# Decoder kernel: exponentials three steps ahead in the scan layer, and the last expert layer's first two experts split by ScalarE and VectorE

## The chip, the core and the metric

The kernel is one program on one core of a Trainium2 chip. The core has five engines with a queue of instructions each: TensorE (PE) for matrix products and transposes, VectorE (DVE), ScalarE (ACT), GpSimd (POOL), and SyncE (SP), which here only starts transfers. They wait for each other through semaphores. The metric is the device time of one execution in microseconds (us), the median of some runs.

## The reference

Two sequences of 1024 tokens, 256 channels wide, go through six layers, each behind a layer norm and added to its input. The change touches the first and the last:

```python
# x: (2, 1024, 256)
x = x + L0_attn(layernorm(x))    # a selective state-space scan ("Mamba"), inner width 512, 16 states
x = x + L0_xattn(layernorm(x))   # attention to a context of 77 rows
x = x + L0_ffn(layernorm(x))     # top-1 mixture of 8 experts
x = x + L1_attn(layernorm(x))    # a mixer of several parts
x = x + L1_xattn(layernorm(x))   # attention with sparsemax
x = x + L1_ffn(layernorm(x))     # top-2 mixture of 8 experts

# L0_attn, the scan over time t, for each of 512 channels d and 16 states n:
dA = exp(dt_t * A)
h  = dA * h + dt_t * B_t * x_t
y  = einsum('bdn,bn->bd', h, C_t)

# L1_ffn:
m, sel = top_k(logits, 2)        # masks and two softmaxes give two weights for each token
for e in range(8):
    h = silu(x @ w1[e].T) * (x @ w3[e].T)
    out = out + wte[:, e:e+1] * (h @ w2[e].T)
```

## The kernel before, in words

**The scan layer** (`mamba`, from L226). The 2048 tokens are worked in NK = 4 chunks of 512, and each chunk in NU = 64 steps: 16 states n by CI = 4 groups c of 128 channels. One step is one tile of 128 channels x 512 tokens, and step G of the whole layer passes through four engines:

- ScalarE makes the exponential dA[G] (`decay`, L582), into one of AR = 6 buffers. For that it waits until the scan of step G - 6 has read its buffer. It also makes the B product UT, tokens on the partitions and all 512 channels in a row, in four slices of 128 tokens for a state (`times_b`, L572). The slices for the group of four steps N are made during the four steps of group N - 1; the first of them waits until TensorE has taken the slices of group N - 2 out of the same buffer.
- TensorE turns UT into channels by tokens in one of UR = 2 PSUM banks (`bring_u`, L418). It can begin a group's first step only when all four slices of the group are there, and a bank is free when the scan two steps back has read it.
- VectorE runs the scan h = dA*h + u along the 512 tokens (L741), into one of HR = 8 buffers H.
- GpSimd multiplies H by C (`times_c`, L841, buffers HC, YR = 8), and TensorE adds the products up in PSUM (`sum_up`, L427), LAG = 5 steps behind.

What each engine does within a chunk is an order written out by hand. On ScalarE (L610 to L640) step p holds one slice of B product, then the exponential of step p, and at some steps a burst of other work: at p = 14 four SiLU for the next chunk, at 19, 20 and between 21 and 31 copies and magnitudes, at 37 two SiLU of the gate and four logarithms of the next chunk, at 43 two more SiLU, and at 49, 53, 57 and 59 a column copy DTXT for the next chunk each. SiLU, exponential and logarithm lie in different tables, so bursts hold table loads. The loop before:

```python
for p in range(NU):
    if k * NS + p // CI + 1 < NK * NS:
        times_b(k * NS + p // CI + 1, p % CI)
    if k or p >= AR:
        decay(k * NU + p)
```

The six exponentials of the first chunk's start are made before the loop. GpSimd, too, has other work within a chunk (convolution, products by x, logarithm corrections for the next chunk).

**The last layer** (`ffn1`, from L1651). A router (TensorE's logits, then some fifty small operations on VectorE, L1884 to L1947, with two exponentials on ScalarE, L1853) gives each token two slots among MB = 39 blocks of 128 rows, each block belonging to one expert. GpSimd then scatters the rows with 32 indirect writes (L1762) into the DRAM table `rows_in`, which 13 plain transfers of 384 KB on SyncE's queue (L1709) have filled with zeros before. SyncE loads each block back (DI, L1717), TensorE transposes it (L1793), ScalarE and VectorE copy it as a high and a low part (L1857, L1952), and TensorE multiplies it by the expert's weights in three passes of two-part products (L145 to L147). The results go to `rows_out`, and a last gather (L1777) adds them to the tokens.

The weights of an expert are three parts of 1 MB (128 partitions x 2048 values each), w1, w3 and w2. Each part is loaded into one of three staging buffers and split into a high part, rounded to fp32r (L1749), and a low part, the rest (L1751). The parts are counted p = 0 to 23 over all eight experts. GpSimd does all of it before the change: it issues a load, rounds, subtracts, and issues the load for the same staging buffer three parts on. W has room for two experts, and expert e >= 2 is split once the blocks of expert e - 2 are done. GpSimd's order, after the zeros are set:

```python
for p in range(3): load(p)
split(0)             # expert 0
pool.wait_ge(slots_ready, 1)   # the routing is done
pool.wait_ge(cleared, ...)     # the 13 writes of zeros have landed
... 32 indirect writes ...
split(1)             # expert 1
```

`lo_ready` counts the finished low parts; TensorE waits for it before an expert's first product.

## Time and profile before

| | us |
|---|---|
| median of three timed runs | 2108.66 (2106.80 to 2109.61) |
| the profiled execution | 2104.53 |
| span of its trace | 2102.6 |
| busy: TensorE products, weight loads | 1544.3, 1291.4 |
| busy: VectorE, GpSimd, ScalarE | 1113.8, 949.6, 911.8 |

The mean granted TensorE clock of the profiled execution is 0.868 of full speed. The places of the trace that matter here, in us from the start of the span:

| stretch | from | to |
|---|---|---|
| scan layer, first chunk | 59.76 | 189.18 |
| second chunk | 189.18 | 319.5 |
| third chunk | 319.5 | 448 |
| fourth chunk | 448 | 545 |
| last layer | 1559.8 | 2102.6 |
| its layer norm on ScalarE | | 1568.2 |
| its routing on VectorE | 1577.59 | 1612.81 |
| its scatter on GpSimd | 1613.73 | 1654.4 |
| its first expert block on TensorE | 1661.7 | |
| its last gather on GpSimd | 2052 | |

A row of the timeline gives the start, the duration, the engine, the line, the operation, the tiles out<-in with their shapes and how many instructions run back to back in it; in brackets stands how long the engine was idle just before and whose result ended that ("<-DMA" is a landing, "DVEq" the queue of VectorE, "issue" no wait that the trace shows). A row of waits gives who waited (engine, tile, line) for whom, the total, the number of waits and the longest. A row of windows gives a stretch, its length, and for TensorE's products, its weight loads, VectorE, ScalarE and GpSimd the busy us and the count, then the mean granted clock, the busy share of the DMA engines and the GB/s they moved. A row by line gives the shortest, median and longest duration in ns, the first and the last start in us, and the shape.

### The profile page before, as it was taken

The page shows a single profiled execution, that of the slowest core. Times are in us where ns is not written, and L with a number is a line of the kernel's source. Part 1 is how long each engine was busy: PE and PEld are TensorE (multiplying, and loading weights), DVE is VectorE, ACT ScalarE, POOL GpSimd, SP SyncE. Part 2 cuts the span into 40 slices and gives each one's busy share as a digit, 9 for nine tenths or more (in the row PEclk, how much of TensorE's full clock was granted, in tenths as well). Part 3 has the DMA queues.
Part 4 walks back from the last instruction along what each step waited for, and adds up shares of the span by engine and source line. Part 5 has one row for each costly group of instructions (what it writes and reads, how often), then busy time and mean ns, then how long its engine had stood idle before and what let it go on. Part 6 is the DMA issues. An engine that isn't in the chain of part 4 may idle for free. (4 is left out here: it accounts for less than half of the span.)

```text
span 2102.6 us, 28530 instructions
## 1 busy us (share of the span) xinstructions
PE 1544.3 (73%) x9844; PEld 1291.4 (61%) x9844; DVE 1113.8 (53%) x2193; ACT 911.8 (43%) x1602; POOL 949.6 (45%) x743
## 2 busy tenths in 40 slices
PE   4887878878689738721269995977890399989990
PEld 1556555667568738710159984964880288878880
DVE  6667867688669513255674447447736032322322
ACT  4696886979444415421062227534230132322220
POOL 0598795998433345530042116030025805594406
PEclk8899999999899869955579996999895699999995
DMA  3001001011210325210000001020033312333003
GB/s 114 21 22 41 37 25 41 21 41 41 67 27 1 121 84 190 82 40 1 29 20 2 1 1 43 1 82 0 1 113 133 105 51 68 109 128 104 28 18 122
DMA packets 51960, 114.46 MB, mean 54 GB/s; under 512 B 13996, under 2 KB 34377, under 8 KB 44276
## 3 DMA queue, kind: packets, MB, share of 16 engines
q1 hardware_dynamic: 43764, 75.23, 10.2%
q0 software_dynamic: 8064, 37.45, 5.3%
q8 instruction: 85, 1.39, 0.3%
q14 instruction: 47, 0.39, 0.1%
HBM read 87.02 MB, written 25.87 MB: 54 GB/s over the span
## 5 line engine op out<-in xcount | busy, mean ns | idle before, releaser
L841 POOL TENSOR_TENSOR HC<-H,CB 128x512 f32<-128x512 f32 x256 | 321.9, 1277 | 107.4 <-DVE H L741 96.5
L418 PE MATMUL ps<-ident,UT 128*128 128x128 f32 x1024 | 168.1, 289 | 50.2 <-DVE H L741 40.1
L572 ACT ACTIVATE UT<-DTXT,BT 128x512 f32<-128x512 f32 x256 | 181.3, 711 | 44.3 <-PE ps L418 43.8
L741 DVE TENSOR_TENSOR_SCAN H<-dA,ps 128x512 f32<-128x512 f32 x128 | 154.8, 1217 | 84.4 <-PE ps L418 38.5
L418 PEld LDWEIGHTS ps<-ident,UT 128*128 128x128 f32 x1024 | 123.4, 147 | 123.1 <-DVE H L741 59.2
L582 ACT ACTIVATE dA<-DT,nA 128x512 f32<-128x512 f32 x256 | 181.0, 709 | 2.8 <-DVE DT L709 2.7
L741 DVE TENSOR_TENSOR_SCAN H<-dA,HL,ps 128x512 f32<-128x512 f32 x128 | 159.2, 1274 | 40.8 <-ACT dA L582 23.6
L427 PE MATMUL ps<-ident,HC 128*128 128x128 f32 x1024 | 159.4, 284 | 26.9 <-POOL HC L841 25.5
L1749 POOL TENSOR_TENSOR f_W<-f_stage,f_zeros 128x2048 fp32r<-128x2048 f32 x24 | 86.6, 3607 | 144.7 <-POOLq L1769 138.5
L427 PEld LDWEIGHTS ps<-ident,HC 128*128 128x128 f32 x1024 | 123.7, 147 | 35.0 <-POOL HC L841 34.5
L1966 DVE TENSOR_TENSOR f_XN<-f_XN,ps 128x1024 f32<-128x1024 f32 x39 | 47.6, 1221 | 173.3 <-PE ps L147 173.3
L145 PE MATMUL ps<-f_W,f_DIT 128*128 x312 | 128.4, 412 | 8.8 <-POOL f_W L1751 7.1
L147 PE MATMUL ps<-f_W,f_DIT 128*128 x312 | 124.8, 400 | 0.0
L146 PE MATMUL ps<-f_W,f_DIT 128*128 x312 | 124.7, 400 | 0.0
L1751 POOL TENSOR_TENSOR f_W<-f_stage,f_W 128x2048 fp32r<-128x2048 f32 x24 | 110.3, 4595 | 1.9
L1959 DVE TENSOR_TENSOR f_HT<-ps,f_HT 128x512 fp32r<-128x512 f32 x78 | 50.3, 686 | 100.9 <-ACT f_HT L1863 100.9
L1520 POOL TENSOR_TENSOR f_l<-f_w,f_h 128x2048 fp32r<-128x2048 f32 x16 | 73.5, 4594 | 63.9 <-ACT f_h L1581 63.2
L1874 ACT ACTIVATE f_EO<-ps 128x256 f32<-128x256 f32 x39 | 14.9, 383 | 179.7 <-PE ps L147 179.7
L138 PE MATMUL ps<-ident,h_XN 128*128 128x128 f32 x96 | 29.4, 432 | 84.6 <-DVE h_XN L96 59.1
L145 PE MATMUL ps<-f_W,f_HT 128*128 x312 | 87.7, 281 | 1.7 <-issue 1.7
L146 PE MATMUL ps<-f_W,f_HT 128*128 x312 | 87.8, 281 | 0.0
L147 PE MATMUL ps<-f_W,f_HT 128*128 x312 | 87.7, 281 | 0.0
(490 smaller groups left out, 4284.3 us busy)
## 6 DMA issues: line engine op xcount, KB each, us to landing
f_stage<-in_f_w POOLq DMA_DIRECT2D x24, 1024.0 KB, 5.5
CB<-m_c_rows SPq DMA_DIRECT2D x16, 1024.0 KB, 4.6
f_w<-in_f_w SPq DMA_DIRECT2D x16, 1024.0 KB
f_rows_in<-f_zeros SPq DMA_DIRECT2D x13, 384.0 KB, 13.7
f_DI<-f_rows_in SPq DMA_DIRECT2D x39, 128.0 KB
f_rows_out<-f_EO SPq DMA_DIRECT2D x39, 128.0 KB, 2.0
a_values<-a_zeros SPq DMA_DIRECT2D x8, 320.0 KB, 5.4
a_VBD<-a_values SPq DMA_DIRECT2D x8, 320.0 KB, 4.4
```

The costliest lines, as they stand in the source:

```text
L145: pe.matmul(out, ah, bh, start=first, stop=False)
L146: pe.matmul(out, ah, bl, start=False, stop=False)
L147: return pe.matmul(out, al, bh, start=False, stop=last)
L418: ins = pe.transpose(PS[4 + G % UR][:, t * P:(t + 1) * P], UT[:, n % 2, t, c * P:(c + 1) * P], g.ident[:, :])
L427: ins = pe.matmul(PS[t][:, c * P:(c + 1) * P], HC[:, G % YR, t * P:(t + 1) * P], g.ident[:, :], start=False, stop=(u == NU - 1), is_transp ...
L572: act.activation(UT[:, N % 2, t, :], DTXT[:, k % 2, t, :], ACT.Copy, scale=BT[:, k % 2, t, n:n + 1]).then_inc(ut_ready, 1)
L582: act.activation(dA[:, G % AR, :], DT[:, k % 2, c, :], ACT.Exp, scale=nA[:, c, n:n + 1]).then_inc(da_ready, 1)
L741: dve.tensor_tensor_scan(H[:, G % HR, :], dA[:, G % AR, :], PS[4 + G % UR][:, :], first, ALU.mult, ALU.add).then_inc(h_ready, 1)
L841: pool.tensor_tensor(HC[:, y, :], H[:, s, :], CB[:, n // 4 % CR, n % 4, :], ALU.mult).then_inc(hc_ready, 1)
L1520: pool.tensor_tensor(l[:, e % 2, :, :], w[:, e % WR, :, :], h[:, e % 2, :, :].bitcast(F32), ALU.subtract).then_inc(wl_ready, 1)
L1749: pool.tensor_tensor(hi, stage[:, q, :], zeros[:, 0:1].to_broadcast([P, PART]), ALU.add).then_inc(hi_ready, 1)
L1751: pool.tensor_tensor(lo, stage[:, q, :], hi.bitcast(F32), ALU.subtract).then_inc(lo_ready, 1)
```

## The change

In the scan layer the call for the exponential names the step three further on (LEAD = 3), both in its number and in the condition that keeps out the six made ahead and those behind the last step. The B products, the bursts and all that the other engines do stay where they are. Since `decay(G)` waits for scan G - 6, the exponential that stands at step p now waits for scan p - 3.

In the last layer the weights of experts 0 and 1 no longer pass through GpSimd. SyncE issues their six loads: parts 0 to 2 ahead of the writes of zeros, parts 3 to 8 behind them, each when the low part three parts earlier is done (parts 6 to 8 belong to expert 2). ScalarE rounds expert 0's three parts behind its share of the layer norm, and expert 1's behind the two exponentials of the router. VectorE makes the six low parts behind the routing, right after it has told GpSimd that the slots are ready. GpSimd goes from the zeros straight to the wait for the slots, and splits from expert 2 on as before.

```diff
@@ mamba @@
+LEAD = 3
...
                     for p in range(NU):
                         if k * NS + p // CI + 1 < NK * NS:
                             times_b(k * NS + p // CI + 1, p % CI)
-                        if k or p >= AR:
-                            decay(k * NU + p)
+                        if AR <= k * NU + p + LEAD < NK * NU:
+                            decay(k * NU + p + LEAD)
@@ ffn1 @@
-        chain, wg_loaded, w_loaded = sem("chain"), sem("wg_loaded"), [sem(f"w_loaded{i}") for i in range(3)]
+        chain, wg_loaded = sem("chain"), sem("wg_loaded")
+        w_first, w_loaded = ([sem(f"{n}{i}") for i in range(3)] for n in ("w_first", "w_loaded"))
...
+        def high_part(p):
+            at = (p // 3 % 2) * 2 * WSZ + p % 3 * PART
+            return W[:, at:at + PART]
+
+        def low_part(p):
+            at = (p // 3 % 2) * 2 * WSZ + WSZ + p % 3 * PART
+            return W[:, at:at + PART]
...
                 sp.dma_start(rt.wg[:, :, :], a["f1_wg"]).then_inc(wg_loaded, 16)
+                for q in range(3):
+                    sp.dma_start(stage[:, q, :], a[WPARTS[q]][0]).then_inc(w_first[q], 16)
                 sp.wait_ge(zeroed, 1)
                 for q in range(MB // 3):
                     sp.dma_start(rows_in[q * 3 * P:(q + 1) * 3 * P, :].rearrange("(p r) d -> p (r d)", r=3),
                                  zeros[:, :]).then_inc(cleared, 16)
+                for p in range(3, 9):
+                    sp.wait_ge(lo_ready, p - 2)
+                    sp.dma_start(stage[:, p % 3, :], a[WPARTS[p % 3]][p // 3]).then_inc(w_first[p % 3], 16)
                 sp.wait_ge(scattered, 16 * 2 * NT)
...
                     for q in range(3):
                         p = 3 * e + q
...
-                        pool.wait_ge(w_loaded[q], 16 * (e + 1))
+                        hi, lo = high_part(p), low_part(p)
+                        if e == 2:
+                            pool.wait_ge(w_first[q], 16 * 3)
+                        else:
+                            pool.wait_ge(w_loaded[q], 16 * (e - 2))
...
-                for p in range(3):
-                    load(p)
                 pool.wait_ge(zeroed, 1)
-                split(0)
                 pool.wait_ge(slots_ready, 1)
                 pool.wait_ge(cleared, 16 * (MB // 3))
...
-                split(1)
+                pool.wait_ge(lo_ready, 6)
                 for e in range(2, E):
...
             def _(act):
+                def split_high(e):
+                    for q in range(3):
+                        act.wait_ge(w_first[q], 16 * (e + 1))
+                        act.activation(high_part(3 * e + q), stage[:, q, :], ACT.Copy).then_inc(hi_ready, 1)
+
                 ln.act(act)
+                split_high(0)
                 for q in range(2):
                     act.wait_ge(rt.exp_in, q + 1)
                     act.activation(rt.EX[:, :, :], rt.L[:, :, :], ACT.Exp).then_inc(rt.exp_out, 1)
+                split_high(1)
...
                 dve.sem_inc(slots_ready, 1)
+                for p in range(6):
+                    dve.wait_ge(hi_ready, p + 1)
+                    dve.tensor_tensor(low_part(p), stage[:, p % 3, :], high_part(p).bitcast(F32), ALU.subtract).then_inc(lo_ready, 1)
```

**ScalarE at the end of the first chunk.** The rows are its instructions in order. DTXT is the column copy at step 59, UT the slices of B products, dA the exponentials; the wait m_dt_ready marks an exponential of the next chunk. Before:

```order
L555 ACTIVATE DTXT<-ps 128x4x128 [waits m_dtxt_full]
L572 ACTIVATE UT<-DTXT,BT 128x512 [waits m_u_ready,m_dtxt_ready,m_bt_ready]
L582 ACTIVATE dA<-DT,nA 128x512 [waits m_h_ready]
L572 ACTIVATE UT<-DTXT,BT 128x512
L582 ACTIVATE dA<-DT,nA 128x512 [waits m_h_ready]
L572 ACTIVATE UT<-DTXT,BT 128x512
L582 ACTIVATE dA<-DT,nA 128x512 [waits m_h_ready]
L572 ACTIVATE UT<-DTXT,BT 128x512
L582 ACTIVATE dA<-DT,nA 128x512 [waits m_h_ready]
L572 ACTIVATE UT<-DTXT,BT 128x512 [waits m_u_ready]
L582 ACTIVATE dA<-DT,nA 128x512 [waits m_h_ready,m_dt_ready]
```

And with the change, from the same column copy on:

```order
L556 ACTIVATE DTXT<-ps 128x4x128 [waits m_dtxt_full]
L573 ACTIVATE UT<-DTXT,BT 128x512 [waits m_u_ready,m_dtxt_ready,m_bt_ready]
L583 ACTIVATE dA<-DT,nA 128x512 [waits m_h_ready]
L573 ACTIVATE UT<-DTXT,BT 128x512
L583 ACTIVATE dA<-DT,nA 128x512 [waits m_h_ready,m_dt_ready]
L573 ACTIVATE UT<-DTXT,BT 128x512
L583 ACTIVATE dA<-DT,nA 128x512 [waits m_h_ready,m_dt_ready]
L573 ACTIVATE UT<-DTXT,BT 128x512
L583 ACTIVATE dA<-DT,nA 128x512 [waits m_h_ready,m_dt_ready]
L573 ACTIVATE UT<-DTXT,BT 128x512 [waits m_u_ready]
L583 ACTIVATE dA<-DT,nA 128x512 [waits m_h_ready,m_dt_ready]
```

The next chunk's first exponential was the fifth behind the column copy and is now the second; the slices of B products have kept their places.

**ScalarE at the start of the last layer.** XT are the layer norm's copies, f_r_EX the router's two exponentials, f_DIT the first copies of block rows. Before:

```order
L110 ACTIVATE f_ln_std<-f_ln_mv,eps 128x16
L119 ACTIVATE XT<-ps 128x2x128 x16
L1853 ACT_TABLE_LOAD
L1853 ACTIVATE f_r_EX<-f_r_L 128x128 x2
L1857 ACTIVATE f_DIT<-ps 128x256 x2
L1869 ACT_TABLE_LOAD
```

And with the change, where f_W<-f_stage is the rounding of three weight parts:

```order
L110 ACTIVATE f_ln_std<-f_ln_mv,eps 128x16
L119 ACTIVATE XT<-ps 128x2x128 x16
L1867 ACTIVATE f_W<-f_stage 128x2048 x3
L1873 ACT_TABLE_LOAD
L1873 ACTIVATE f_r_EX<-f_r_L 128x128 x2
L1867 ACTIVATE f_W<-f_stage 128x2048 x3
L1878 ACTIVATE f_DIT<-ps 128x256 x2
L1890 ACT_TABLE_LOAD
```

Three roundings stand between the layer norm and the router's first exponential, and three more between its second exponential and the first block's rows.

**GpSimd at the start of the last layer.** f_stage<-in_f_w is the load of a weight part, f_rows_in<-f_XN,f_idx the scatter. Before:

```order
L1734 IOTA f_blk 128x39
L1740 DMA f_stage<-in_f_w 128x2048 x3
L1749 TENSOR_TENSOR f_W<-f_stage,f_zeros 128x2048
L1751 TENSOR_TENSOR f_W<-f_stage,f_W 128x2048
L1740 DMA f_stage<-in_f_w 128x2048
L1749 TENSOR_TENSOR f_W<-f_stage,f_zeros 128x2048
L1751 TENSOR_TENSOR f_W<-f_stage,f_W 128x2048
L1740 DMA f_stage<-in_f_w 128x2048
L1749 TENSOR_TENSOR f_W<-f_stage,f_zeros 128x2048
L1751 TENSOR_TENSOR f_W<-f_stage,f_W 128x2048
L1740 DMA f_stage<-in_f_w 128x2048
L1762 DMA f_rows_in<-f_XN,f_idx 4992x256 x32
```

And with the change:

```order
L1399 MEMSET f_r_first 128x8
L1749 IOTA f_blk 128x39
L1776 DMA f_rows_in<-f_XN,f_idx 4992x256 x32
L1781 TENSOR_LOAD f_tabi
L1781 ISA x2
L1782 REGISTER_ALU
L1766 TENSOR_TENSOR f_W<-f_stage,f_zeros 128x2048
L1768 TENSOR_TENSOR f_W<-f_stage,f_W 128x2048
```

Nothing stands between GpSimd's constants and the scatter any more, and the first rounding behind it is that of expert 2.

**VectorE at the end of the routing.** f_tabi<-f_tab is the last operation of the routing, f_DIT the low part of the first block's rows. Before:

```order
L1945 TENSOR_SCALAR f_tab<-f_tab 128x40
L1946 COPY f_tab<-f_ends 128x8
L1947 CAST f_tabi<-f_tab 128x80
L1952 TENSOR_TENSOR f_DIT<-ps,f_DIT 128x256 x2
L1966 TENSOR_TENSOR f_XN<-f_XN,ps 128x1024
```

And with the change:

```order
L1966 TENSOR_SCALAR f_tab<-f_tab 128x40
L1967 COPY f_tab<-f_ends 128x8
L1968 CAST f_tabi<-f_tab 128x80
L1972 TENSOR_TENSOR f_W<-f_stage,f_W 128x2048 x6
L1976 TENSOR_TENSOR f_DIT<-ps,f_DIT 128x256 x2
L1990 TENSOR_TENSOR f_XN<-f_XN,ps 128x1024
```

The six subtractions have come in between the routing and the first block.

## Rows read from the trace of the kernel before

**Rows 1.** Windows view, first chunk: us, busy by engine (count), clock, DMA, GB/s.
```profile
59.76:189.18 129.42, 103.31 (x610) 76.91 (x609) 92.11 (x90) 101.10 (x159) 106.77 (x108) 0.88 0.07 25
```

**Rows 2.** Waits, 70 to 560 us: who for whom, total us, times, longest.
```profile
DVE H L741 <- ACT dA L582: 61.5, 34, 7.1
```

**Rows 3.** Timeline, GpSimd in the scan: start, us, instruction, [idle before <- releaser].
```profile
141.61 1.28 POOL L841 TENSOR_TENSOR HC<-H,CB 128x512 f32<-128x512 f32 x1 [0.74 <-DVE H L741]
...
270.69 2.51 POOL L841 TENSOR_TENSOR HC<-H,CB 128x512 f32<-128x512 f32 x2 [1.30 <-DVE H L741]
...
403.41 1.28 POOL L841 TENSOR_TENSOR HC<-H,CB 128x512 f32<-128x512 f32 x1 [0.69 <-DVE H L741]
```

**Rows 4.** Timeline, VectorE, steps 23 and 24 of the first chunk.
```profile
109.91 2.45 DVE L741 TENSOR_TENSOR_SCAN H<-dA,ps 128x512 f32<-128x512 f32 x2 [0.49 <-ACT dA L582]
```

**Rows 5.** Timeline, TensorE, steps 16 and 17 of the first chunk.
```profile
93.51 1.12 PE L418 MATMUL ps<-ident,UT 128*128 128x128 f32 x4 [0.17 <-ACT UT L572]
...
97.28 0.66 PE L418 MATMUL ps<-ident,UT 128*128 128x128 f32 x4
```

**Rows 6.** Timeline, step 60 of the first chunk: VectorE, then TensorE.
```profile
182.66 1.22 DVE L741 TENSOR_TENSOR_SCAN H<-dA,ps 128x512 f32<-128x512 f32 x1 [3.34 <-ACT dA L582]
...
180.21 1.06 PE L418 MATMUL ps<-ident,UT 128*128 128x128 f32 x4
```

**Rows 7.** Timeline, last chunk, step 37 on: ScalarE, then VectorE.
```profile
498.24 0.71 ACT L582 ACTIVATE dA<-DT,nA 128x512 f32<-128x512 f32 x1
...
503.89 0.70 ACT L572 ACTIVATE UT<-DTXT,BT 128x512 f32<-128x512 f32 x1
...
504.19 3.73 DVE L741 TENSOR_TENSOR_SCAN H<-dA,HL,ps 128x512 f32<-128x512 f32 x3 [3.52 <-ACT dA L582]
...
515.36 5.15 DVE L741 TENSOR_TENSOR_SCAN H<-dA,HL,ps 128x512 f32<-128x512 f32 x4 [3.06 <-ACT dA L582]
```

**Rows 8.** Timeline, last layer's routing: VectorE, then GpSimd.
```profile
1577.59 3.81 DVE L1885 TENSOR_SCALAR f_AB<-f_r_PL 128x128 f32<-128x128 f32 x1
1581.43 4.59 DVE L1886 TENSOR_TENSOR f_AB<-f_AB,f_r_PL 128x128 f32<-128x128 f32 x1
...
1586.38 4.14 DVE L1891 TENSOR_TENSOR f_r_A<-f_AB,f_m 128x128 f32<-128x128 f32 x1
1590.55 4.52 DVE L1898 TENSOR_TENSOR f_r_L<-f_r_PL,f_m 128x128 f32<-128x128 f32 x1
...
1600.46 0.29 DVE L1893 TENSOR_TENSOR f_r_L<-f_r_PL,f_m 128x128 f32<-128x128 f32 x1
...
1581.38 4.49 POOL L1751 TENSOR_TENSOR f_W<-f_stage,f_W 128x2048 fp32r<-128x2048 f32 x1
```

**Rows 9.** Timeline, last layer's scatter: VectorE, GpSimd, TensorE.
```profile
1612.61 0.20 DVE L1947 CAST f_tabi<-f_tab 128x80 int32<-128x80 f32 x1
...
1613.73 1.07 POOL L1762 DMA_INDIRECT f_rows_in<-f_XN,f_idx  x1 [17.95 <-DVEq L1948]
...
1658.10 0.69 PE L1793 MATMUL ps<-ident,f_DI 128*128 128x128 f32 x2 [53.14 <-DMA f_DI<-f_rows_in]
```

**Rows 10.** Timeline, the last gather: VectorE, then GpSimd.
```profile
2063.99 3.25 DVE L1974 SCALAR_TENSOR_TENSOR X<-f_W,f_mult,X 128x256 f32<-128x256 f32 x8 [18.39 <-DMA f_W<-f_rows_out,f_idx]
...
2066.45 1.28 POOL L1777 DMA_INDIRECT f_W<-f_rows_out,f_idx  x1 [0.30 <-issue]
2068.03 1.00 POOL L1777 DMA_INDIRECT f_W<-f_rows_out,f_idx  x1 [0.30 <-issue]
```

**Rows 11.** Instructions of a line: ns min/median/max, first and last start, shape.
```profile
L1293 DVE TENSOR_TENSOR a_PN<-a_SC,a_th x16: 1423/1424/1443, 1471.5 to 1545.3; 128x1232 f32<-128x1232 f32 x16
...
L1581 ACT ACTIVATE f_h<-f_w x8: 1904/1904/1944, 726.9 to 868.1; 128x2048 fp32r<-128x2048 f32 x8
```

**Rows 12.** Windows view, last layer, while weights and zeros move.
```profile
1566.00:1570.00 4.00, 4.00 (x36) 3.62 (x35) 0.96 (x3) 3.48 (x9) 1.39 (x1) 1.00 0.99 407
```

**Rows 13.** Timeline, GpSimd before the third expert's split.
```profile
1758.54 3.59 POOL L1749 TENSOR_TENSOR f_W<-f_stage,f_zeros 128x2048 fp32r<-128x2048 f32 x1 [76.65 <-POOLq L1769]
```

More of the change, by code:

```diff
@@ L1745, in split @@
                         p = 3 * e + q
-                        hi = W[:, (e % 2) * 2 * WSZ + q * PART:(e % 2) * 2 * WSZ + (q + 1) * PART]
-                        lo = W[:, (e % 2) * 2 * WSZ + WSZ + q * PART:(e % 2) * 2 * WSZ + WSZ + (q + 1) * PART]
-                        pool.wait_ge(w_loaded[q], 16 * (e + 1))
+                        hi, lo = high_part(p), low_part(p)
[3 more added lines that the diff above has]
+                            pool.wait_ge(w_loaded[q], 16 * (e - 2))
                         pool.tensor_tensor(hi, stage[:, q, :], zeros[:, 0:1].to_broadcast([P, PART]), ALU.add).then_inc(hi_ready, 1)
```

## The prediction, made before the change was run

> **What bounds the kernel now.** The kernel is a row of stages on one core, and the change touches two of them, so I read the windows view by stage, then the waits, then the timeline at the places where a wait ends. The scan layer takes 485 of the 2102.6 us (four chunks, 59.8 to 545). In the first chunk no engine is full over the chunk: GpSimd has 106.8 busy us of 129.4, ScalarE 101.1, TensorE 103.3, VectorE 92.1 [rows 1]. The bound passes from one to the next within a chunk: VectorE up to step 14, TensorE and ScalarE together up to about 24, GpSimd from there on. VectorE waits 61.5 us in the layer for exponentials, 34 times [rows 2]. That is a ceiling, not a gain: what counts is only the part of it that reaches GpSimd, or VectorE where VectorE is the bound.
>
> In the last expert layer the time up to the first expert product is a serial chain: layer norm, router logits, routing on VectorE, 32 indirect row writes on GpSimd, load, transpose. TensorE stands still for 53.1 us in it [rows 9]. Behind it come 39 blocks in which TensorE is hardly ever idle, and whatever the chain gains moves them forward as a whole.
>
> **The scan layer, part by part.** Removed and added work: none; every exponential and B product stays. On ScalarE the exponential for step p+3 now stands where that of step p stood. Three scans that follow ScalarE's pace take 3.73 us [rows 7], so a step is 1.24 and the lead is worth at most 3.7 us to VectorE. The B products cap it: a scan needs its transposed B product, whose fourth slice is made at the end of the group of four steps before. What VectorE gains at a burst is therefore to be read at the next multiple of four.
>
> Entry into GpSimd's part (steps 15 to 24): the 5 us wait at step 15 shrinks, but TensorE already begins step 16 at 93.51 straight behind the B product, and comes to step 17 only at 97.28, with its own queue in between [rows 5]. Those times don't move. The exponential ends last only at step 23, by 0.49 us [rows 4]. I take 0.5 us in each of three chunks: 1.5 us.
>
> The burst at step 37 (two SiLU, four logarithms, three table loads): VectorE stands 7 us, but GpSimd has work in its queue and waits only 0.74, 1.30 and 0.69 us in the three chunks [rows 3]. With steps 38 and 39 free to run during the burst these waits go: 2.7 us.
>
> The end of a chunk: at step 60 ScalarE hangs at a column copy, and VectorE waits 3.34 us for the exponential; from there VectorE is the bound. What is late next is TensorE's transpose for step 60, which ends at 180.21 + 1.06 = 181.27 [rows 6]. With 0.2 us from its end to the scan, step 60 starts at 181.45 instead of 182.66: 1.2 us, three times, 3.6 us.
>
> The last chunk has no next chunk's work on GpSimd, and its two bursts are felt: 3.52 and 3.06 us of wait [rows 7]. After the change steps 38 and 39 run in the burst, and step 40 waits for the slice at 503.89 + 0.70, plus 0.66 for the transpose and 0.2: 505.4, against 504.19 + 2 x 1.23 = 506.65 now. That is 1.2 us; the second burst starts at a group's end (step 43) and gives a little more, but ScalarE itself has not moved, so the two don't add up. I take 1.5 us.
>
> Sum for the scan layer: 1.5 + 2.7 + 3.6 + 1.5 = 9.3 us. Bounds: 0 if each of these gains is handed back at the next chunk's TensorE or GpSimd part, and 21 if VectorE kept all three steps (3.7 us) at the three chunk ends and the two last bursts (18.5) plus the 2.7.
>
> New waits: each exponential now waits for the scan three steps back, at every step; queued behind it are the B products and all the bursts. A B product at a group's start already waited for a transpose that needs the same scan, so no wait is longer there. In the last burst ScalarE starts the exponential at 498.24; VectorE ended step 37 at 504.19 - 3.52 = 500.67, so step 34, for which the moved one waits, ended by 497.0 [rows 7]. It costs nothing while ScalarE is no more than three steps ahead.
>
> **The last layer, part by part.** GpSimd loses six roundings of about 3.6 us, six subtractions of about 4.5 and six load issues. What this frees is VectorE: four routing operations of 128x128 take 3.81, 4.59, 4.14 and 4.52 us while GpSimd splits weights, and another of the same size and kind takes 0.29 once it is done; the second ends at 1586.02, 0.15 behind GpSimd's subtraction [rows 8]. They sit out GpSimd's instruction. Freed: 17.06 - 4 x 0.29 = 15.9 us, all on the chain, since the routing ends at 1612.81 and GpSimd starts its first write at 1613.73 [rows 9].
>
> ScalarE's three roundings for expert 0 take 1.90 us each [rows 11], 5.7 in all, from 1568.2, where its layer norm part ends, to about 1574; then the table load of 1.28. The router's first exponential is wanted after five routing operations of 0.29 behind 1577.59 [rows 8], at about 1579. Hidden, with 3 us to spare, if the weights have landed: 3 MB at some 400 GB/s are 8 us from 1561 on [rows 12]. The 13 clearing writes (5 MB) now stand behind them on SyncE's queue and end near 1583, before GpSimd needs them at 1597. If that cover went, each us is one on the chain.
>
> VectorE's six subtractions come behind the routing. Of two operands in SBUF, 128x1232 takes 1.42 us [rows 11], so 128x2048 some 2.3: six are 14 us. VectorE has no other work until the first block, 42 us later, so for VectorE they are hidden. SyncE's six later loads wait for them one by one and hold its next load, which waits for the scatter anyway; ScalarE's second three roundings end about 15 us after the routing, long before its first copy of rows.
>
> But GpSimd issues its 32 row writes at the same time. No row shows these two together; the nearest is the last gather, where eight VectorE operations of two SBUF operands run back to back for 3.25 us, and one issue takes 1.28 instead of 1.00 [rows 10]. The 0.28 fits an issue that waits for the VectorE operation in flight (0.48 long) and then goes ahead. With operations of 2.3 us and issues every 1.3, each VectorE operation then costs GpSimd 2.3 - 1.3 = 1.0, and the first of the second three up to 1.6: 6.7 us. Lower bound, 0.28 each: 1.7. Upper bound, GpSimd shut out for all of it: 14. I take 6.7, by that row. The layer gains 15.9 - 6.7 = 9.2 us, between 1.9 and 14.2.
>
> The Trainium skill (page "SBUF — State Buffer", section "Who interferes with whom") says that a VectorE instruction with two SBUF inputs shuts out only a GpSimd instruction that reads SBUF, and infers that descriptor generation is not hit by it. By the rule alone the six subtractions would cost nothing and the kernel would come to 2083.5; the 1.28 above speaks against "nothing", and no run here shows it for long operations.
>
> Expert 1's weights leave GpSimd after the scatter (27 us there before). This saves nothing on the path: GpSimd next sits 76.65 us waiting for expert 0's blocks [rows 13].
>
> **Sum.** 9.3 + 9.2 = 18.5 us. The profiled execution took 2104.5 (span 2102.6), which would give 2086.0; it is 4.1 below the median of the three timed runs, 2108.66, against which the change is timed. Forecast: 2108.7 - 18.5 = 2090.2.
>
> **Rivals.** (B) The lead is worth its three steps: 21 us in the scan, 30 in all, 2078.5. For it: the large waits on exponentials. Against: the B slices' cap. (C) The six subtractions shut the scatter out wholly: last layer 1.9, sum 11.2, 2097.5. For it: rows 8, where VectorE waits out whole instructions. Against: rows 10. (D) The scatter is not held at all: 15.9 + 9.3, 2083.5. (E) The lead does nothing, since TensorE's or GpSimd's queue takes the gain back in each chunk: 9.2 alone, 2099.5. For it: rows 5. (F) Slower: the wait at every step keeps ScalarE from running to its group's end ahead of a burst. It decides where ScalarE would be more than three steps ahead of VectorE; two steps of 1.28 lost at each of eleven bursts are 28 us, less 9.2: 2127.5. Against: the 1.2 us of slack worked out above.
>
> **How the numbers follow.** Forecast (2082 to 2098) 0.55, B 0.09, C 0.12, D 0.09, E 0.10, F 0.05. A difference below 0.2% (4.2 us) can't be told from none in this kernel. Nearly all of the first five lie under 2104.4: faster 0.90; same 0.06, where E and C come together; slower 0.04. Range 2076 to 2103: B and D are in, F is out.
>
> **What would show it.** Right: the four routing operations at 0.3 us each, the routing's end 16 us earlier; issues of the scatter beside VectorE's subtractions at up to 2.3 us, six in number, the rest at 1.0; GpSimd's three waits at step 38 gone; step 60 of a chunk behind TensorE instead of ScalarE. Wrong: SiLU or logarithm bursts that start later than now, an exponential of the router behind the roundings, or clearing writes that land after the routing.

## The result, and the profile after

The changed kernel takes 2089.22 us (median of four, 2087.18 to 2089.83) against 2108.22 us (2106.80 to 2109.61): the ratio is 0.9908, 95% interval 0.9891 to 0.9925, so 19.0 us less (15.8 to 23.0). Forecast were 18.5 less. The profiled execution of the changed kernel took 2089.83 and has a span of 2087.8 us, 14.8 below that of before; where the other 4 us of the two profiles' difference are is told below.

**Scan layer.** Waits from 70 to 560 us, same columns and window as [rows 2], in the changed kernel (all lines of `mamba` stand one further on, so L741 is now L742):

```profile
DVE H L742 <- PE ps L419: 84.9, 82, 5.5
...
ACT dA L583 <- DVE H L742: 8.6, 8, 1.3
...
DVE H L742 <- ACT dA L583: 5.7, 8, 2.1
```

VectorE's 61.5 us of waits for exponentials are down to 5.7. Most of it (45 us) is now a wait for TensorE's transposes (84.9 us; before it was 39.8). So the view says what the prediction's first paragraph warned of: 56 us of waits are gone and the layer is some 10 us shorter. The new wait, ScalarE's exponential for a scan, costs ScalarE 8.6 us in 8 places (before: none). The waits of GpSimd at step 38 in [rows 3] are gone: in each chunk the product stands inside a run or behind a copy of 0.2 us without any idle time. GpSimd's timeline, second chunk, then third:

```profile
264.33 4.94 POOL L842 TENSOR_TENSOR HC<-H,CB 128x512 f32<-128x512 f32 x4
...
391.87 4.96 POOL L842 TENSOR_TENSOR HC<-H,CB 128x512 f32<-128x512 f32 x4
```

**Last layer.** VectorE's timeline from the routing on. The rows answer to [rows 8, 9]; the first four are the routing's start, then comes its last operation, then the six new subtractions:

```profile
1570.05 0.23 DVE L1906 TENSOR_SCALAR f_AB<-f_r_PL 128x128 f32<-128x128 f32 x1
1570.31 0.29 DVE L1907 TENSOR_TENSOR f_AB<-f_AB,f_r_PL 128x128 f32<-128x128 f32 x1
...
1570.95 0.29 DVE L1912 TENSOR_TENSOR f_r_A<-f_AB,f_m 128x128 f32<-128x128 f32 x1
1571.28 0.29 DVE L1919 TENSOR_TENSOR f_r_L<-f_r_PL,f_m 128x128 f32<-128x128 f32 x1
...
1589.11 0.20 DVE L1968 CAST f_tabi<-f_tab 128x80 int32<-128x80 f32 x1
1589.46 6.70 DVE L1972 TENSOR_TENSOR f_W<-f_stage,f_W 128x2048 fp32r<-128x2048 f32 x3
1599.13 2.29 DVE L1972 TENSOR_TENSOR f_W<-f_stage,f_W 128x2048 fp32r<-128x2048 f32 x1 [2.98 <-ACT f_W L1867]
1602.90 2.29 DVE L1972 TENSOR_TENSOR f_W<-f_stage,f_W 128x2048 fp32r<-128x2048 f32 x1 [1.48 <-ACT f_W L1867]
1606.43 2.29 DVE L1972 TENSOR_TENSOR f_W<-f_stage,f_W 128x2048 fp32r<-128x2048 f32 x1 [1.24 <-ACT f_W L1867]
```

The four operations that took 17.06 us are at 0.23 to 0.29 us. And GpSimd's timeline, the first ten of the 32 row writes:

```profile
1590.29 2.43 POOL L1776 DMA_INDIRECT f_rows_in<-f_XN,f_idx  x1 [36.75 <-DVEq L1969]
1593.02 1.79 POOL L1776 DMA_INDIRECT f_rows_in<-f_XN,f_idx  x1 [0.31 <-issue]
1595.12 1.88 POOL L1776 DMA_INDIRECT f_rows_in<-f_XN,f_idx  x1 [0.30 <-issue]
1597.31 0.97 POOL L1776 DMA_INDIRECT f_rows_in<-f_XN,f_idx  x1 [0.30 <-issue]
1598.58 0.97 POOL L1776 DMA_INDIRECT f_rows_in<-f_XN,f_idx  x1 [0.30 <-issue]
1599.86 2.41 POOL L1776 DMA_INDIRECT f_rows_in<-f_XN,f_idx  x1 [0.30 <-issue]
1602.58 0.97 POOL L1776 DMA_INDIRECT f_rows_in<-f_XN,f_idx  x1 [0.30 <-issue]
1603.85 2.19 POOL L1776 DMA_INDIRECT f_rows_in<-f_XN,f_idx  x1 [0.31 <-issue]
1606.34 0.97 POOL L1776 DMA_INDIRECT f_rows_in<-f_XN,f_idx  x1 [0.30 <-issue]
1607.62 1.95 POOL L1776 DMA_INDIRECT f_rows_in<-f_XN,f_idx  x1 [0.30 <-issue]
```

Six writes of 1.8 to 2.4 us, one for each subtraction, the other 26 at 0.97. Hold the rows side by side: the first subtraction ends at 1589.46 + 6.70/3 = 1591.7, the write in flight at 1592.72; the fourth ends at 1601.42, the write at 1602.27; the fifth at 1605.19, the write at 1606.04. A write that starts while a subtraction runs ends 0.85 to 1.0 us behind that subtraction's end. One that had begun before the subtraction (1598.58, 1602.58, 1606.34) takes its 0.97.

Both layers by their steps, from the timelines of all engines. "scan layer" is the first scan's start to the last product of GpSimd, "between" from there to GpSimd's first instruction in the last layer, "to logits" from there to the copy of the logits (L1884), "routing" from there to the last cast's end, "scatter" the first write's start to the last one's end, "load" from there to the first expert product, "blocks" to the last product. The third and fourth number columns are two experiments that stand below:

```
us          before   changed   lead only   last layer only
scan layer  484.27    474.09      473.08            483.57
between    1015.81   1018.28     1016.95           1015.97
to logits    17.44     17.45       17.44             17.44
routing      35.55     19.59       35.92             19.58
scatter      40.70     47.39       40.70             47.30
load          7.24      7.24        7.09              6.99
blocks      387.27    388.00      388.62            388.36
```

The three rows that the change touches give -10.2, -16.0 and +6.7: 19.5 us. The rest of the program is the same code and came out 4.6 us longer in this profile of after than in that of before, above all between the two layers (2.5 us) and in the last gather (1.2). Over all profiles of this study the stretch between the layers goes from 1014.5 to 1019.8 us without any edit in it. So the 14.8 us between the two profiles holds 4.6 us of such spread, and the touched rows' 19.5 us go with the 19.0 us of the medians.

### The profile page after: what moved, and what is told of

The parts are those of the page before. It is cut to its first block and busy times, and to the rows that moved or that the text cites. A ratio compares the mean times of both kernels' runs of the same rounds, so it can differ in the third digit from the quotient of the medians.

```text
span 2087.8 us, 28529 instructions
## 1 busy us (share of the span) xinstructions
PE 1537.9 (74%) x9844; PEld 1286.0 (62%) x9844; DVE 1119.0 (54%) x2199; ACT 922.5 (44%) x1608; POOL 902.4 (43%) x722
## 5 line engine op out<-in xcount | busy, mean ns | idle before, releaser
L742 DVE TENSOR_TENSOR_SCAN H<-dA,ps 128x512 f32<-128x512 f32 x128 | 152.7, 1213 | 78.2 <-PE ps L419 67.2
L583 ACT ACTIVATE dA<-DT,nA 128x512 f32<-128x512 f32 x256 | 181.4, 710 | 11.4 <-DVE H L742 8.6
L742 DVE TENSOR_TENSOR_SCAN H<-dA,HL,ps 128x512 f32<-128x512 f32 x128 | 158.3, 1270 | 36.6 <-PE ps L419 29.9
L1766 POOL TENSOR_TENSOR f_W<-f_stage,f_zeros 128x2048 fp32r<-128x2048 f32 x18 | 64.9, 3605 | 167.0 <-POOLq L1783 166.7
L1768 POOL TENSOR_TENSOR f_W<-f_stage,f_W 128x2048 fp32r<-128x2048 f32 x18 | 83.0, 4614 | 1.4
```

Of the source, the lines that this page charges most:

```text
L583: act.activation(dA[:, G % AR, :], DT[:, k % 2, c, :], ACT.Exp, scale=nA[:, c, n:n + 1]).then_inc(da_ready, 1)
L742: dve.tensor_tensor_scan(H[:, G % HR, :], dA[:, G % AR, :], PS[4 + G % UR][:, :], first, ALU.mult, ALU.add).then_inc(h_ready, 1)
L1766: pool.tensor_tensor(hi, stage[:, q, :], zeros[:, 0:1].to_broadcast([P, PART]), ALU.add).then_inc(hi_ready, 1)
L1768: pool.tensor_tensor(lo, stage[:, q, :], hi.bitcast(F32), ALU.subtract).then_inc(lo_ready, 1)
```

## Experiments

**Each part alone.** The edit of the first is the lead's two lines in the kernel before; of the second, `LEAD = 3` to `LEAD = 0` in the changed kernel.

> The scan layer's part alone: the exponentials three steps ahead, the last layer as before. My theory gives 9.3 us less than before (the trace of the changed kernel ends the scan layer's last product by C 10.0 us earlier), about 2099, and a last layer whose routing and scatter are as before (35.5 us from the copy of the logits to the last cast, 40.7 us from the first indirect write to the last). If the lead does nothing by itself (rival E): 2108. If the three steps are kept whole (rival B): 2087.

> The last layer's part alone: LEAD = 0, so the scan layer is as before. My theory gives 15.9 us from the routing less 6.7 us of a stretched scatter, 9.2 us less than before, about 2099. If the scatter's stretch came from something in the other part, the scatter would be back at 40.7 us here and the time at 2092; if the two parts only add up by chance, the sum of this run's and the other part's gain is not the 19 us of both.

Both expectations count from the 2108 us of before; in this set of runs it was 2106.22. Measured: the lead alone 2094.79 us, ratio 0.9947 (0.9933 to 0.9961), 11.4 us less by the medians; the last layer alone 2098.30, ratio 0.9963 (0.9950 to 0.9977), 7.9 less. The sum, 19.3, and the 19.0 of both together can't be told apart; nor can each part from its forecast (9.3 and 9.2), since the intervals are 3 us wide to either side. The table above has both traces: each part moves its own rows, the untouched rows differ by up to 1.4 us, and the scatter is stretched by 6.6 us without the lead too.

**Where in the chunk.** From the starts of scans and products I took the time between fixed steps, the mean of the two kernels without lead less the mean of five with LEAD = 3 (the changed kernel, the lead alone, and three of the experiments below):

```
gain in us                                chunk 1   2      3      4     sum   forecast
step 14 to product 24 (entry)                0.26   1.62   0.24    -    2.1        1.5
product 37 to product 38                     0.74   1.33   0.72    -    2.8        2.7
product 59 to the next chunk's step 3        0.86   1.18   1.80    -    3.8        3.6
last chunk, step 24 to the end                 -      -      -   1.96   2.0        1.5
all else                                                                -0.1        0
```

**How many steps of lead.** The edit is the number in `LEAD = 3`.

> The changed kernel with LEAD = 1. My theory says that one exponential ahead is nearly enough, since the B products' slices cap the rest: GpSimd's waits at step 38 need step 38's exponential only, the chunk end is held by TensorE's transpose for step 60, and in the last chunk step 40 waits for its slice whatever the lead. So the scan layer takes at most 1.5 us more than with LEAD = 3 (473 us), and the time is 2087 to 2090, like the changed kernel. If the gain goes with the steps of lead (rival B's reading), a third of 10.6 us is left: the scan layer at 480, the time at 2094.

> The changed kernel with LEAD = 4: the exponential at step p waits for scan p - 2. With 5 the SiLU burst at step 14 of the second chunk began 5.4 us later than with 3, and the scan layer took 487 us against 473. The wait is one scan shorter here: the burst 2.7 us later than with 3, of which 1.7 us is time in which the burst itself waited for VectorE's columns. I expect 1 to 4 us more than LEAD = 3, the scan layer at 474 to 477, the time at 2088 to 2092. If the cost sets in all at once at 5: 473.

> The changed kernel with LEAD = 5: the exponential at step p waits for scan p - 1, so ScalarE goes in step with VectorE (my rival F, which the lead of 3 was said to stay clear of). In that state the fourth slice of a group is made only behind scan 4N - 2, and the transpose for step 4N (0.7 to 1.06 us) behind it: some 0.7 us of VectorE in each group where VectorE is the bound, 3.5 groups at the start of each chunk and 16 in the last, about 20 us more than LEAD = 3: 2107. If the wait costs nothing even then, 2087 or less.

Measured: with LEAD = 1 2087.46 us (2085.91 to 2090.34), ratio 0.9916 (0.9899 to 0.9932), a scan layer of 473.43. One exponential ahead gives all that three give, although VectorE still waits for exponentials for long (view of waits, 70 to 560 us):

```profile
DVE H L742 <- ACT dA L583: 46.9, 28, 6.0
```

That is 46.9 of the 61.5 us, and 5.7 with LEAD = 3. This is the sharpest test of the step on the B products' slices: what the lead is worth is set by the transposes that come behind them and not by how many exponentials lie ready. LEAD = 4 gives 2089.26 (0.9901 to 0.9934 of before) and 475.28, within the 474 to 477 expected; its time can't be told from LEAD = 3. LEAD = 5 gives 2107.88 (median of ten, 2101.44 to 2110.62; ratio 1.0009, 0.9999 to 1.0019): the whole gain is gone, that of the last layer too. The time is the expected one, but the trace bears out only a part of it: the scan layer takes 486.96, 13.7 us more than with LEAD = 3 where 20 were expected, and the profiled execution was the fastest of the ten, 6.4 us below their median. Where those 6.4 us lie is not shown. The place was half right. I had expected a stall in every group where VectorE is the bound, from step 3 to 14 of a chunk; there the second chunk takes 27.5 us with either lead. The loss is at the entry of the second chunk (23.95 instead of 18.59), at the ends of two chunks (2.3 and 2.2) and in the last chunk (3.3). Waits with LEAD = 5, 60 to 560 us, then ScalarE's timeline at the burst of step 14 in the second chunk:

```profile
ACT dA L583 <- DVE H L742: 64.4, 84, 2.5
```

```profile
220.14 0.73 ACT L583 ACTIVATE dA<-DT,nA 128x512 f32<-128x512 f32 x1 [1.28 <-DVE H L742]
220.88 1.28 ACT L519 ACT_TABLE_LOAD   x1
```

The same place with LEAD = 3 (the lead alone):

```profile
214.71 0.73 ACT L583 ACTIVATE dA<-DT,nA 128x512 f32<-128x512 f32 x1 [1.34 <-DVE H L742]
215.45 1.28 ACT L519 ACT_TABLE_LOAD   x1
```

The burst begins 5.4 us later (6.0 counted from the chunk's first scan), since the exponential ahead of it waits for scan p - 1 instead of p - 3, and everything behind it on ScalarE, B products included, is later by what is left of that. It is rival F; it is seen in the trace at 4 and in the time at 5. ScalarE's waits for a scan (70 to 560 us) grow with the lead: 8.6 us in 8 places with 3, 25.7 in 25 with 4, 62.5 in 82 with 5.

**Slices of B products in pairs.**

```diff
-                        if k * NS + p // CI + 1 < NK * NS:
-                            times_b(k * NS + p // CI + 1, p % CI)
+                        if k * NS + p // CI + 1 < NK * NS and p % CI < 2:
+                            for t in range(2):
+                                times_b(k * NS + p // CI + 1, p % CI * 2 + t)
```

> The changed kernel with the B products' slices made in pairs, two at the first and two at the second step of each group of four, none at the third and fourth; LEAD stays 3. If the slices cap what the lead is worth (my step on the prediction's steps 40 and 60), a burst at step 37 finds the group of step 40 complete, VectorE runs through three more steps and the scan layer ends 2 to 5 us earlier: 2085 to 2087. If TensorE's transposes or ScalarE's own busy time are what comes next, it is the same, 2089. Slower, if the pairs hold back the exponential at each group's start: 2092.

Measured: 2085.85 us, ratio 0.9904 (0.9889 to 0.9919), and a scan layer of 471.47 against 472.5 to 474.1 in the six profiles with LEAD = 3, so 1.1 to 2.6 us less where I expected 2 to 5. It does not come from where I looked for it. In the last chunk step 40 starts 24.8 us behind step 24, as without the pairs (24.7). The slices are there, but step 39's transpose stands in TensorE's queue behind input products (w_in) that wait for ScalarE's copies ZT, part of the burst:

```profile
491.05 1.13 PE L347 MATMUL ps<-w_in,XT 128*128 128x512 f32 x2 [2.25 <-ACT ZT L524]
```

In the first three chunks VectorE's step 40 does come 1.4 to 2.8 us earlier, counted from step 24, and GpSimd's product of it hardly moves (0.1 us). The gain lies in the first 24 steps of the first chunk (0.7 us), at the second chunk's entry (0.5) and in smaller bits. So the cap on slices is not the only one: with it lifted, TensorE's order gives the same step 40. In the time the pairs can't be told from the changed kernel (0.9908); the scatter took 48.51 us in this profile, 1.1 more.

**Who stretches the row writes.**

> Expert 0's three subtractions on VectorE stand between the layer norm and the router's logits, where it waits 10.3 us for TensorE (three of 2.24 us need 6.7); expert 1's split is GpSimd's again, behind the scatter, as before the change. The scatter then runs beside no VectorE operation. My theory: its 32 writes are back at 40.7 us instead of 47.4, the time is 6.7 us below the changed kernel, about 2082.5. Rival: the stretch comes from the weight loads that land during the scatter, or from the scatter's earlier start: then it stays near 47 us and 2089. Rival: the last subtraction ends after the logits are there and holds the routing by up to 1 us.

```diff
@@ VectorE @@
                 ln.dve(dve)
+                for p in range(3):
+                    dve.wait_ge(hi_ready, p + 1)
+                    dve.tensor_tensor(low_part(p), stage[:, p % 3, :], high_part(p).bitcast(F32), ALU.subtract).then_inc(lo_ready, 1)
...
-                for p in range(6):
...
@@ GpSimd, behind the scatter @@
-                pool.wait_ge(lo_ready, 6)
+                split(1)
```

(ScalarE's second three roundings go, and SyncE issues parts 3 to 5 only.) Measured: 2079.77 us, ratio 0.9873 (0.9858 to 0.9888), by the ratios 7.4 us below the changed kernel where 6.7 were expected. The scatter takes 40.71 us, its first write 1.09 (1.07 in the kernel before), the others 0.97 to 0.99. This run takes the weight loads out of the scatter's time as well; the next one keeps them. With the version that adds the pairs (below) it is the best of the study. VectorE's timeline where the three subtractions stand now, in [rows 8]' place:

```profile
1560.02 6.70 DVE L1902 TENSOR_TENSOR f_W<-f_stage,f_W 128x2048 fp32r<-128x2048 f32 x3 [3.06 <-ACT f_W L1867]
1567.27 0.29 DVE L1907 COPY f_r_PL<-ps 128x128 f32<-128x128 f32 x1 [0.56 <-PE ps L1406]
```

They end 0.56 us before the logits come, so they are hidden, and nothing holds the routing (19.58 us).

> The changed kernel with each of VectorE's six subtractions of 128x2048 cut into four of 128x512, so the same work in 24 operations of about 0.6 us. My mechanism (a write's issue waits for the VectorE operation in flight and then goes ahead, ending 0.85 us behind its end): the cost goes with the length of one operation, at most 0.3 us for a write and 1 to 3 us in all, the scatter at 42 to 44 us, the time 4 to 5 us below the changed kernel. If the cost goes with VectorE's busy time, or comes from the weight loads that run at the same time: 47.4 us as now and no gain.

```diff
+                part = PART // 4
                 for p in range(6):
                     dve.wait_ge(hi_ready, p + 1)
-                    dve.tensor_tensor(low_part(p), stage[:, p % 3, :], high_part(p).bitcast(F32), ALU.subtract).then_inc(lo_ready, 1)
+                    for i in range(4):
+                        at = slice(i * part, (i + 1) * part)
+                        ins = dve.tensor_tensor(low_part(p)[:, at], stage[:, p % 3, at], high_part(p)[:, at].bitcast(F32), ALU.subtract)
+                    ins.then_inc(lo_ready, 1)
```

Measured: 2082.74 us, ratio 0.9891 (0.9875 to 0.9908), by the ratios 3.6 us below the changed kernel; the scatter 44.77 us where 42 to 44 were expected. Nine writes are longer than 0.97, by 0.26 to 0.53 us each. So the cost goes down with the length of one operation (4.1 us instead of 6.7, for a little more VectorE time), but less than I expected: each write that meets VectorE pays up to one short operation, and with short operations more writes meet one. The weight loads run at the same time in this kernel and the changed one alike, so they don't make the difference.

> The changed kernel, but expert 0's three subtractions are plain copies of the staged weights (one operand in SBUF), and each of expert 1's three is four subtractions of 128x512 whose second operand lies in PSUM; so both experts' low parts are left out, and their place and size kept. What is read is the row of GpSimd's 32 writes. If only operations with two SBUF operands hold the descriptor writes: no write above 1.1 us and the scatter at 40.7 us. If any VectorE operation with SBUF data holds them: the first writes 1.5 to 2.4 us long as in the changed kernel. I expect the copies to hold them (the routing's one-operand operation of the kernel before was held by GpSimd too, 3.81 us), the ones with PSUM not (the scans of the first layer, one operand in SBUF and one in PSUM, run at 1.22 us beside GpSimd's products).

```diff
-                    dve.tensor_tensor(low_part(p), stage[:, p % 3, :], high_part(p).bitcast(F32), ALU.subtract).then_inc(lo_ready, 1)
+                    if p < 3:
+                        dve.tensor_copy(low_part(p), stage[:, p % 3, :]).then_inc(lo_ready, 1)
+                        continue
+                    for i in range(4):
+                        at = slice(i * part, (i + 1) * part)
+                        ins = dve.tensor_tensor(low_part(p)[:, at], stage[:, p % 3, at], PS[2][:, 0:part], ALU.subtract)
+                    ins.then_inc(lo_ready, 1)
```

One execution, 2085.30 us; its result is not the kernel's, since both experts' low parts are left out. The scatter takes 41.87 us. VectorE, then GpSimd:

```profile
1590.46 3.51 DVE L1974 CAST f_W<-f_stage 128x2048 fp32r<-128x2048 f32 x3
1598.73 2.48 DVE L1978 TENSOR_TENSOR f_W<-f_stage,ps 128x512 fp32r<-128x512 f32 x4 [4.76 <-ACT f_W L1867]
...
1591.29 1.66 POOL L1776 DMA_INDIRECT f_rows_in<-f_XN,f_idx  x1 [36.63 <-DVEq L1969]
1593.26 1.57 POOL L1776 DMA_INDIRECT f_rows_in<-f_XN,f_idx  x1 [0.31 <-issue]
...
1598.96 0.98 POOL L1776 DMA_INDIRECT f_rows_in<-f_XN,f_idx  x1 [0.30 <-issue]
```

The copies, with one operand in SBUF, hold two writes. The subtractions with one operand in SBUF and one in PSUM hold none (all other writes 0.97 or 0.98), with the weight loads running beside them; of the same size with both operands in SBUF (quarters, above) they cost 0.26 to 0.53 for a write that met one.

**Who stretches the routing.**

> The changed kernel, with three operations of 128x2048 added on GpSimd that start behind VectorE's fifth routing operation and do nothing for the result: a memset (no operand in SBUF), a copy (one), a subtraction (two). This puts the suspected cause of the four stretched routing operations back alone, with no weight loads on GpSimd's queue. My theory: the routing operations in flight during the subtraction take up to 4.5 us instead of 0.29, those beside the memset 0.29; beside the copy I don't know, between 0.29 and its own length. If loads or ScalarE's roundings had been the cause in the kernel before: all at 0.29 and a routing of 19.6 us as in the changed kernel.

```diff
+                pool.wait_ge(rt.exp_in, 1)
+                pool.memset(dst.bitcast(F32), 0.0).then_inc(tried, 1)
+                pool.wait_ge(tried, 2)
+                pool.tensor_copy(dst, src.bitcast(F32)).then_inc(tried, 1)
+                pool.wait_ge(tried, 3)
+                pool.tensor_tensor(dst, src.bitcast(F32), src.bitcast(F32), ALU.subtract).then_inc(tried, 1)
```

One execution, 2097.06 us. GpSimd's three operations, then VectorE's of the same time:

```profile
1573.61 1.80 POOL L1756 MEMSET f_HT<- 128x2048 f32 x1 [19.87 <-DVE f_r_L L1930]
1575.48 1.89 POOL L1758 CAST f_HT<-f_HT 128x2048 fp32r<-128x2048 f32 x1
1577.45 3.60 POOL L1760 TENSOR_TENSOR f_HT<-f_HT 128x2048 fp32r<-128x2048 f32 x1
...
1573.84 1.65 DVE L1934 TENSOR_SCALAR f_MK<-f_r_A 128x128 f32<-128x128 f32 x1
1575.52 1.99 DVE L1939 TENSOR_TENSOR f_r_A<-f_r_EX,f_MK 128x128 f32<-128x128 f32 x1
1577.54 0.28 DVE L1940 TENSOR_REDUCE f_t<-f_r_A 128x16 f32<-128x128 f32 x1
...
1578.15 3.04 DVE L1944 TENSOR_TENSOR f_r_A<-f_r_PL,f_m 128x128 f32<-128x128 f32 x1
```

With the suspected cause alone put back, VectorE's operations are long again, each to within 0.15 us of the end of GpSimd's, and the routing takes 25.45 us instead of 19.6. That no loads are needed for it is shown. I had expected 0.29 us beside the memset, and it was 1.65.

**Both improvements.** Early subtractions and slices in pairs:

> Both changes that gained: expert 0's subtractions ahead of the routing, expert 1's split behind the scatter, and the B products in pairs. If they add up: 2079.8 of the first alone less the 1.4 to 2.6 us by which the pairs ended the scan layer earlier, 2077.5 to 2078.5. If the pairs' gain was a difference between two profiles of the same code (the changed scan layer took 473.1 to 474.1 us in three of them), 2079.8.

Measured: 2079.37 us (2077.44 to 2080.91), ratio 0.9876 (0.9860 to 0.9893). The trace has the scan layer at 471.21 and the scatter at 40.70, so both edits do what they did alone; in the time the pairs' 2 us don't show. Whether they are lost in the spread or given back behind (the last layer's blocks took 390.3 us in this profile, 387.3 to 388.9 in all others) stays open.

## Why the prediction held, step by step

- **Routing: forecast 15.9 us, measured 16.0** (35.55 to 19.59). That VectorE's operation ended 0.15 us behind GpSimd's in [rows 8] was the right thing to read, and the row of 0.29 us for the same operation the right price. The last experiment shows the cause by putting it back.
- **The scatter's stretch: 6.7, measured 6.7** (40.70 to 47.39). The row that carried it, an issue of 1.28 us in [rows 10], was a weak one, and its model holds in kind: an issue that starts beside an operation waits it out. Its terms (1.0 us for each, 1.6 for the first of the second three) add up to 6.6, and the rows of after show 1.46, 0.82 and 0.91 for the first three subtractions, 1.44, 1.22 and 0.98 for the others. That the two sums meet within 0.1 us is luck: with the same six subtractions the scatter took 46.99 to 48.56 us in seven profiles, a stretch of 6.3 to 7.9, since a write pays for what is left of the subtraction beside which it starts (the longest took 3.06). With short operations the model promised 1 to 3 us and 4.1 came.
- **The rival that the scatter isn't held (D)** rested on the Trainium skill too, and the writes of 1.8 to 2.4 us beside subtractions with two SBUF operands speak against it. The Trainium skill (page "SBUF — State Buffer", section "Who interferes with whom") infers that such an instruction leaves descriptor generation alone; for indirect writes these 6.7 us are against the inference. Why they are held stays open. An indirect write also reads its list of rows from SBUF (f_idx in its rows), so the other half of the rule that the prediction quoted, on a GpSimd instruction that reads SBUF, may be enough; no run here has issues without such a list beside these subtractions. What the same section says of the other forms agrees with these runs: an operation with one input in SBUF and one in PSUM holds nothing (0.97 us a write), a copy can and here does (1.66 and 1.57), and a reduction beside GpSimd's subtraction takes its 0.28.
- **ScalarE's roundings: hidden, as forecast.** The router's first exponential still waits 4.31 us for VectorE behind them, and the writes of zeros had landed well before the scatter, as the DMA engines' share in the windows shows (0.11, then 0.00). ScalarE's timeline (its table load of 1.28 us, left out here, follows the roundings), then two windows:

```profile
1560.40 5.59 ACT L1867 ACTIVATE f_W<-f_stage 128x2048 fp32r<-128x2048 f32 x3
...
1571.60 0.31 ACT L1873 ACTIVATE f_r_EX<-f_r_L 128x128 f32<-128x128 f32 x1 [4.31 <-DVE f_r_L L1919]
...
1575.00:1580.00 5.00, 0.00 (x0) 0.00 (x0) 4.37 (x16) 0.31 (x1) 0.00 (x0) 0.50 0.11 44
1580.00:1590.00 10.00, 1.22 (x4) 0.93 (x4) 7.50 (x30) 0.00 (x0) 0.00 (x0) 0.50 0.00 1
```

- **Step 38: 2.7, measured 2.8.** GpSimd's three waits of [rows 3] were the gain itself, chunk by chunk (0.74, 1.33, 0.72 for 0.74, 1.30, 0.69).
- **Chunk ends: 3.6, measured 3.8, by other steps than the forecast's, so the agreement is luck.** Step 60 of the first chunk starts at 180.00, not at 181.45: TensorE's transpose takes 0.60 us instead of 1.06 and comes earlier. But of the 2.7 us at step 60 some 0.9 are left at the next chunk's step 3. What takes most of the rest is the hold-up of the routing again, for which the prediction had no term here. VectorE has four layer norm operations (m_XN) between its scans. One takes 0.38 us, the others 1.05, 1.47 and 1.46, and each of these three ends 0.15 us behind a GpSimd product that runs beside it (182.19, 186.14 and 188.65 behind 182.04, 185.99 and 188.50). In the kernel before it was one of the four (1.15 us). TensorE, then VectorE:

```profile
179.26 0.60 PE L419 MATMUL ps<-ident,UT 128*128 128x128 f32 x4
...
180.00 1.22 DVE L742 TENSOR_TENSOR_SCAN H<-dA,ps 128x512 f32<-128x512 f32 x1 [0.76 <-PE ps L419]
181.13 1.05 DVE L666 TENSOR_SCALAR m_XN<-X,m_mv,m_rstd 128x256 f32<-128x256 f32 x1
182.11 1.21 DVE L742 TENSOR_TENSOR_SCAN H<-dA,ps 128x512 f32<-128x512 f32 x1
183.24 0.38 DVE L666 TENSOR_SCALAR m_XN<-X,m_mv,m_rstd 128x256 f32<-128x256 f32 x1
...
184.67 1.47 DVE L666 TENSOR_SCALAR m_XN<-X,m_mv,m_rstd 128x256 f32<-128x256 f32 x1
...
187.20 1.46 DVE L666 TENSOR_SCALAR m_XN<-X,m_mv,m_rstd 128x256 f32<-128x256 f32 x1
```

- **Entries: 1.5, measured 2.1,** and unevenly: 1.6 of it in the second chunk. The forecast took the first chunk's rows for all three. In the second GpSimd itself waited 2.39 us for the scan behind the burst at step 14; that wait is gone, and 1.6 us of it are left at step 24.
- **Last chunk: 1.5, measured 2.0**, of which 1.5 from step 37 on, where it was forecast: 3.5 us at step 38, of which 2.0 fall back, and 0.5 ahead of it. At the first burst the transpose of step 40's slice was the limit, as said: TensorE waits for the slice and VectorE for TensorE. At the second burst, step 45, it was not the slice, which had been made a group earlier: TensorE came to the transpose behind output products (L407) that wait for ScalarE's copies ZT. TensorE, then VectorE:

```profile
496.13 0.66 PE L419 MATMUL ps<-ident,UT 128*128 128x128 f32 x4 [0.89 <-ACT UT L573]
...
504.05 1.13 PE L407 MATMUL ps<-m_w_out,GD 128*128 128x256 f32 x4 [1.16 <-ACT ZT L524]
...
496.93 1.28 DVE L742 TENSOR_TENSOR_SCAN H<-dA,HL,ps 128x512 f32<-128x512 f32 x1 [1.56 <-PE ps L419]
...
505.75 1.28 DVE L742 TENSOR_TENSOR_SCAN H<-dA,HL,ps 128x512 f32<-128x512 f32 x1 [1.74 <-PE ps L419]
```

- **Rivals.** B falls by the scan layer, 10 us shorter and not 21, and by LEAD = 1, which has the whole gain. C and D fall by the scatter of 47.4 us. E falls by the lead alone. F was a real mechanism, and the slack I worked out for it (ScalarE no more than three steps ahead) is what the series shows: no loss at 3, 2 us of scan layer at 4, nearly 14 at 5.

That forecast and result differ by 0.5 us is partly luck: the scan layer came out 1 us better than its terms, two of which were right for other reasons than given, and medians of the kernel before differ by nearly 3 us between two sets of runs (2108.2 and 2105.5).

## What to carry to other kernels

A wait of one engine for another tells the ceiling; what a lead is worth is read at the next thing that the waiting engine needs, here the transposed slice and TensorE's turn to make it, and then one step of lead may be as good as three. In these runs GpSimd's work on SBUF held VectorE's, and VectorE's held GpSimd's indirect writes, so work moved from one to the other goes where GpSimd neither computes nor issues indirect writes, in a stretch in which VectorE waits anyway. A lead that goes through a ring of buffers needs buffers to spare: here, with six buffers, a lead of 5 made the maker run in step with the user, and its bursts of other work came late; 4 cost 2 us, 3 nothing.

## What the runs showed of the hardware

- An indirect write's issue on GpSimd (0.97 us) that starts while VectorE subtracts with both operands in SBUF ends 0.85 to 1.0 us behind that operation; VectorE is not slowed (three in 6.70 us, beside the writes as without them). One already begun isn't held.
- A memset of 1.80 us on GpSimd, which reads nothing, held a VectorE operation with one SBUF operand (0.23 us) for 1.65. I had taken memsets for harmless.
- GpSimd's copy of 1.89 us beside the layer norm of the last layer held the first of VectorE's sixteen operations for 1.38 us instead of 0.40; it ended 0.15 us behind the copy (sixteen in 6.22 us, in the kernel before 5.26).
- GpSimd's products of 128x512 (1.28 us) beside the layer norm operations m_XN (0.38 us) at a chunk's end held three of four for 1.05 to 1.47 us.
